# Sums of squares by ScalarE's accumulator, and a new order of steps, in a gated-memory and routed feed-forward kernel

## The reference

```python
ctx = causal_ema(x, tau_ctx)
wg = sigmoid(concat(x, ctx) @ Wg.T + bg);  gated = x * wg
h1 = gelu(x @ Wn1.T + bn1);  mod = 0.5 + sigmoid(h1 @ Wn2.T + bn2)
traces = causal_ema(gated * mod[..., d], tau_raws[d])   # for each of 128 d
temporal = sum_d traces[d] * softmax(blend)[d]
gate = sigmoid(temporal @ Wtemp.T + btemp)
soma = gelu(x @ Wsoma.T + bsoma)
out = (soma * gate) @ Wout.T
y = (out - out.mean(-1)) / sqrt(out.var(-1) + 1e-5) * gamma + beta
scores = y @ w_router;  top_idx = top 16 of 32 tokens of each sequence
update = sigmoid(top_scores) * (gelu(y[top_idx] @ W1 + b1) @ W2 + b2)
result = x + y.at[top_idx].add(update)
```

## Time and profile before

| | |
|---|---|
| time, median of 3 runs | 190.28 us (189.97 to 190.45) |
| the profiled execution's own time | 190.07 us |
| its span in the profile | 188.0 us |
| TensorE busy, weight loads | 179.4 us (95%), 139.8 us |
| VectorE busy | 142.5 us (76%) |
| GpSimd busy | 132.3 us (70%) |
| ScalarE busy | 94.7 us (50%) |
| DMA | 5.62 MB |
| mean granted TensorE clock | 0.997 |

### The profile page before, as it was taken

The page is one execution under the profiler, slowest core; times in us unless marked ns, Lnnn a source line. Parts: engine busy times, 40 slices in busy tenths (PEclk is TensorE's granted clock), DMA queues, the critical chain, the costliest instruction groups (busy, mean ns, idle before and its releaser), DMA issues.

```text
span 188.0 us, 3687 instructions
## 1 busy us (share of the span) xinstructions
PE 179.4 (95%) x1256; PEld 139.8 (74%) x1256; DVE 142.5 (76%) x247; ACT 94.7 (50%) x172; POOL 132.3 (70%) x142
## 2 busy tenths in 40 slices
PE   6999999999999999999999999999998999997991
PEld 6777485687758677877786889767865997895981
DVE  1687978967977559988888766999799865967632
ACT  3156763645652543363623477394683916637230
POOL 7307126596887999998799889977899478809700
PEclk9999999999999999999999999999999999999998
DMA  4795000000000000000000000000100000303032
GB/s 125 186 250 145 0 2 0 5 0 0 5 0 0 0 0 3 0 0 3 2 0 3 0 0 0 3 2 0 50 11 0 2 3 0 112 3 112 0 108 59
DMA packets 12785, 5.62 MB, mean 30 GB/s; under 512 B 2880, under 2 KB 12640, under 8 KB 12768
## 3 DMA queue, kind: packets, MB, share of 16 engines
q1 hardware_dynamic: 11616, 5.20, 10.2%
q10 hardware_dynamic: 1152, 0.20, 0.6%
HBM read 3.30 MB, written 2.10 MB: 29 GB/s over the span
## 4 chain that ended last, share of the span: by engine, by line
PE 88%; DVE 4%; POOL 3%; issue 2%; ACT 0%; DVEq 0%; POOLq 0%
PE ring L996 28%; PE ring L1063 8%; PE ring L953 4%; PE ring L926 4%; PE ring L969 4%; PE ring L932 4%; PE ring L980 4%; PE ring L1023 4%; PE ring L954 4%; PE ring L1011 3%; PE ring L1003 3%; PE ring L878 2%; PE ring L1047 2%; PE ring L960 2%; PE ring L986 2%
## 5 line engine op out<-in xcount | busy, mean ns | idle before, releaser
L434 POOL TENSOR_TENSOR ctx_acc<-ctx_acc,prod 128x384 f32<-128x384 f32 (+20 forms) x75 | 81.5, 1100 | 26.1 <-DVE prod L772 21.0
L772 DVE TENSOR_TENSOR prod<-ring,gm 128x384 f32<-128x384 f32 (+20 forms) x75 | 41.7, 579 | 12.4 <-PE ring L996 9.1
L996 PE MATMUL ring<-mod_hi,decayed_lo 128*128 128x512 f32 (+12 forms) x104 | 34.6, 370 | 0.0
L996 PE MATMUL ring<-mod_lo,decayed_hi 128*128 128x512 f32 (+12 forms) x104 | 30.0, 326 | 0.0
L996 PE MATMUL ring<-mod_hi,decayed_hi 128*128 128x512 f32 (+12 forms) x104 | 30.0, 326 | 0.0
L996 PEld LDWEIGHTS ring<-mod_hi,decayed_lo 128*128 128x128 f32 x104 | 18.6, 189 | 8.8 <-issue 7.2
L996 PEld LDWEIGHTS ring<-mod_lo,decayed_hi 128*128 128x128 f32 x104 | 19.3, 189 | 1.6 <-issue 0.7
L996 PEld LDWEIGHTS ring<-mod_hi,decayed_hi 128*128 128x128 f32 x104 | 19.2, 189 | 0.9
L759 DVE TENSOR_TENSOR state<-ring,blend_w 128x1024 f32<-128x1024 f32 x16 | 18.8, 1217 | 0.5 <-PE ring L969 0.4
L1063 PEld LDWEIGHTS ring<-w_sb,gm 128*128 128x128 f32 x128 | 14.8, 192 | 1.2 <-issue 1.2
L1063 PE MATMUL ring<-w_sb,gm 128*128 128x128 f32 x128 | 15.2, 276 | 0.1
(11 more groups left out here) (162 smaller groups left out, 375.0 us busy)
## 6 DMA issues: line engine op xcount, KB each, us to landing
x_nat<-in_x_dram SPq DMA_DIRECT2D x3, 512.0 KB, 5.2
out_dram<-x_nat SPq DMA_DIRECT2D x3, 512.0 KB, 3.2
x_nat<-in_x_dram SPq DMA_DIRECT2D x2, 256.0 KB, 4.8
w_sb<-in_L_ffn_W_dram SPq DMA_DIRECT2D x2, 256.0 KB, 4.7
out_dram<-x_nat SPq DMA_DIRECT2D x2, 256.0 KB, 2.3
down<-in_cond_dram SPq DMA_DIRECT2D x2, 64.0 KB, 3.1
prod<-in_L_cond_Wg_dram ACTq DMA_DIRECT2D x1, 128.0 KB, 2.9
prod<-in_L_cond_Wsoma_dram ACTq DMA_DIRECT2D x1, 64.0 KB, 2.9
```

Of the source, the lines that this page charges most:

```text
L434: nc.gpsimd.tensor_tensor(dst, dst, packed(prod[:, n % NP, 0:width(r)], r, k), ALU.add).then_inc(acc_done, 1)
L772: nc.vector.tensor_tensor(dst, packed(slot(step), r, k), lagged(gated(r), r, k), ALU.mult).then_inc(read(step), 1)
L996: last = nc.tensor.matmul(to[:, c], w[:, k, :], src[:, c], start=(i == 0), stop=(i == len(parts) - 1))
```

## The change

Two things change. First, `out` on ScalarE squares each of its four tiles by an instruction of its own, which also sums the squares along the row into `small` (`accum_out`). The step `stats` on VectorE is gone (its names stay in the table and do nothing), and so is its wait; the sums are done when ScalarE is. Second, `ORDER` is replaced by another order of the same steps.

```diff
                 elif kind == "out":
-                    at = nth(step)
-                    if at > 1:
-                        last = [s for s in STEPS if s[0] == "stats"][at - 2]
-                        act.wait_ge(stats_done, nth(last))
-                    nc.scalar.activation(squares[:, :, :].rearrange("p (h n) e -> p h n e", h=2),
-                                         slot(step).rearrange("p (h n) -> p h n", h=2)[:, :, 0:2 * OW].rearrange(
-                                             "p h (n w) -> p h n w", w=OW)[:, :, :, 0:E], ACT.Square,
-                                         scale=E ** -0.5).then_inc(read(step), 1)
+
+                    if nth(step) > 1:
+                        act.wait_ge(stats_done, QT * (nth(step) - 1))
+                    if r >= 2:
+                        act.wait_ge(rstd_done, r - 1)
+                    for n in range(QT):
+                        at = n // 2 * BANK + n % 2 * OW
+                        nc.scalar.activation(squares[:, n, :], slot(step)[:, at:at + E], ACT.Square, scale=E ** -0.5,
+                                             accum_out=small[:, r % 2, 5, k * QT + n:k * QT + n + 1]).then_inc(stats_done, 1)
...
-                elif kind == "stats":
-
-                    dve.wait_ge(read(("out", r, k)), reads_after(("out", r, k)) - 1)
-                    if r >= 2:
-                        dve.wait_ge(norm_done, BEFORE[r - 1] * QT)
-                    nc.vector.tensor_reduce(small[:, r % 2, 5, k * QT:(k + 1) * QT], squares[:, :, :], AX_X,
-                                            ALU.add).then_inc(stats_done, 1)
...
 ORDER = """
-decay:0 turn_a:0 xt:0 context:0 turn_b:0 powers:0 h1:0 wg:0 soft:0 xt:1 gated:0 context:1 turn_c:0 table:0.0
+decay:0 turn_a:0 xt:0 context:0 plus_beta:0 turn_b:0 h1:0 powers:0 wg:0 soft:0 gated:0 xt:1 context:2
...
-up:3.0 score:4 up:3.1 bc:4 normed:4 turn_pick:3 tie:4 pick:4 residual:3 down:3 gather:4 scatter:3 up:4.0
+score:4 normed:4 turn_pick:3 bc:4 tie:4 pick:4 plus_beta:3 residual:3 down:3 plus_beta:4 gather:4 scatter:3
```

More of the change, by code:

```diff
@@ L78 @@
-turn_pick:2 pick:3 sum:4 gate:4 soma_gate:4 residual:2 down:2 gather:3 out:4.0 stats:4.0 var:4 scatter:2
-up:3.0 score:4 up:3.1 bc:4 normed:4 turn_pick:3 tie:4 pick:4 residual:3 down:3 gather:4 scatter:3 up:4.0
-up:4.1 residual:4 turn_pick:4 down:4 scatter:4
+decay:0 turn_a:0 xt:0 context:0 plus_beta:0 turn_b:0 h1:0 powers:0 wg:0 soft:0 gated:0 xt:1 context:2
+turn_c:0 context:1 h1:1 table:0.0 mod:0 split:0 context:4 low:0 xt:2 rw:0 turn_f:0 table:0.1 mod:1 table:0.2
+table:0.3 split:1 early:0 unit:0.0 wg:1 context:3 gated:1 unit:0.3 xt:3 h1:2 low:1 unit:0.8 nat:0.0 early:1
@@ new lines @@
+turn_d:0 unit:0.11 unit:0.12 unit:1.0 unit:0.13 unit:1.12 unit:1.7 unit:1.9 mod:2 plus_beta:1 unit:0.1
+unit:1.6 state:0.0 xt:4 wg:2 gated:2 turn_e:0 unit:0.4 unit:1.4 unit:0.10 unit:0.9 unit:1.13 wg:3 gated:3
+unit:0.6 nat:1.0 h1:4 h1:3 carry:0.0 unit:0.14 unit:0.5 unit:0.15 nat:1.1 back:0.0 unit:1.10 mod:3 unit:0.2
+unit:0.7 split:2 early:2 sum:0 unit:1.5 state:1.0 unit:1.1 soma:0 gate:0 low:2 unit:1.3 soma_gate:0
+carry:1.0 unit:1.8 unit:2.0 nat:2.0 unit:2.15 unit:1.15 unit:1.11 unit:1.14 unit:1.2 unit:2.3 state:2.0
@@ new lines @@
+unit:2.1 split:3 low:3 soma:1 out:0.0 unit:2.8 state:1.1 wg:4 back:1.0 stats:0.0 var:0 carry:2.0 mod:4
+gated:4 score:0 unit:2.11 unit:2.13 unit:2.12 bc:0 carry:1.1 normed:0 tie:0 pick:0 unit:2.6 unit:2.5
+back:2.0 unit:2.14 unit:3.0 nat:2.1 unit:3.1 back:1.1 unit:2.4 early:3 state:2.1 soma:2 sum:1 unit:3.4
+unit:2.10 turn_pick:0 unit:3.14 gather:0 nat:3.1 unit:3.7 nat:3.0 unit:3.12 ffn_w:0 state:3.0 residual:0
+gate:1 soma_gate:1 plus_beta:2 carry:2.1 unit:2.9 unit:2.2 unit:2.7 split:4 up:0.0 low:4 back:2.1 sum:2
@@ new lines @@
+out:1.0 unit:3.2 up:0.1 unit:4.0 unit:4.7 out:1.1 state:3.1 gate:2 unit:4.1 soma_gate:2 early:4 stats:1.0
+stats:1.1 unit:4.9 carry:3.0 unit:3.5 nat:4.0 unit:3.13 out:2.0 state:4.0 var:1 score:1 normed:1 unit:4.15
+down:0 unit:3.15 unit:3.9 unit:3.3 unit:3.6 out:2.1 bc:1 tie:1 soma:4 unit:3.8 carry:3.1 stats:2.0 stats:2.1
+pick:1 var:2 unit:4.13 back:3.0 carry:4.0 gather:1 score:2 soma:3 unit:4.8 back:3.1 unit:3.11 back:4.0
+unit:3.10 unit:4.10 normed:2 sum:3 scatter:0 unit:4.4 unit:4.6 bc:2 up:1.0 turn_pick:1 tie:2 pick:2 gate:3
@@ L81 @@
+residual:1 unit:4.2 unit:4.5 up:1.1 soma_gate:3 gather:2 out:3.0 out:3.1 stats:3.0 unit:4.3 unit:4.12
+stats:3.1 var:3 score:3 up:2.0 normed:3 unit:4.14 down:1 unit:4.11 up:2.1 bc:3 sum:4 scatter:1 turn_pick:2
+tie:3 pick:3 gate:4 soma_gate:4 residual:2 down:2 gather:3 out:4.0 stats:4.0 scatter:2 up:3.0 up:3.1 var:4
+score:4 normed:4 turn_pick:3 bc:4 tie:4 pick:4 plus_beta:3 residual:3 down:3 plus_beta:4 gather:4 scatter:3
+up:4.0 residual:4 up:4.1 turn_pick:4 down:4 scatter:4
 """
```

5 lines of the change are left out of this document (2 added, 3 removed).

## The result

The changed kernel took 194.0 us (median of four executions: 192.73, 192.75, 195.24, 197.64), the kernel before 190.13 beside it. The change is slower, by 1.4 to 2.2%, as forecast. The profiled execution is one of the two of 192.7: span 190.8 us against 188.0.

The account below looks back on a forecast made before the run. TensorE, busy for 95% of the span, was taken to bound the kernel. Start +2.5, middle -0.8 and -0.6, end +2.2 gave +3.3 us, so 193.6 us against the median of 190.28; 8-in-10 range 190.7 to 196.3.

Parts of the forecast that it names:

- The start: `plus_beta:0` waits for `gamma_r` and delays the tables; TensorE waits 2.9 us before its first unit, net +2.5 us.
- +0.5 us before `var:4`: Squares of `out:4` on the path: four ScalarE pairs of 0.46 us, 1.85 us instead of 1.32.
- 4 x 0.27 if the reads overlap: Lower bound for the squares of `out:4`: 1.1 us, so -0.2 us before `var:4`.
- hidden as said: ScalarE's longer squares, 10 us over eight `out` steps, costed at nothing where units on TensorE cover them.
- The middle: The wait before `bc:2` goes, -0.8 us; fewer narrow steps, -0.6 us; new waits costed at nothing.
- -0.6 us: TensorE crosses between step shapes 55 times instead of 61, at 0.11 us each.
- The end: Before `bc:4`: score and spread both held by GpSimd, squares later, `turn_pick:3` filling 0.4 us; +2.2 us.
- two ways in which I let the spread go: Spread of `score:4`: held by gapless GpSimd instructions, tail +2.2 us; or mostly slipping through, +0.1 us.
- Only the start stalls: Rival: the spread of `score:4` gets through between two GpSimd instructions; 191.5 us, chance 0.15.
- new waits in the middle: Rival: `gate:2` or `gate:3` waits for its sum, or ScalarE is late for `down`; 195 to 196.5 us, chance 0.13.
- no difference: Rival: start stall of half the size, net +1.3, spread through, middle as forecast; 190.3 us, chance 0.08.
- Faster: Rival: TensorE's three old waits go and no new one comes; 187.1 us, or some 188; chance 0.11.

Follow-up runs that it names:

- beta0_later: The changed kernel with only `plus_beta:0` moved, from the start to behind the first add (`unit:0.3`): 191.61 us, 1.0056 times the kernel before.
- beta_only_wait: Changed kernel, `plus_beta:3` and `plus_beta:4` moved behind `residual:2`, `gamma_r` given its own semaphore so `plus_beta:0` doesn't wait for it: 188.43 us, 0.9906 times the kernel before.
- acc_only: The kernel before with only the squares summed by ScalarE's accumulator, in the old order: 190.14 us, 0.9997 times the kernel before.
- both_moved: The changed kernel with `plus_beta:0` moved behind `unit:0.3`, and `plus_beta:3` and `plus_beta:4` behind `residual:2`: 188.09 us, 0.9902 times the kernel before.
- residual3_late: `both_moved` with `residual:3` on GpSimd also waiting for the spread of `score:4`: 187.33 us, 0.9847 times the kernel before.
- unit0_behind_wg1: `residual3_late` with `unit:0.0` behind `wg:1` in the table instead of ahead of it: 187.09 us, 0.9846 times the kernel before.
- order_dve_sums: The order of `both_moved` with the old code's sums on VectorE, three `stats` steps set ahead of `out` steps: 188.19 us, 0.9896 times the kernel before.
- both_beta4_late: `both_moved` with `plus_beta:4` alone set behind `var:4` again: 189.34 us, 0.9958 times the kernel before.
- after_again: The changed kernel run once more with nothing edited: 196.74 us, 1.0263 times the kernel before.

## Why the prediction was right, point by point

- **The start.** Right in each step and in its size: line 422 at 16.09 (16.0 forecast), tables at 17.31 (17.3), first unit at 22.55 (22.5), wait 2.37. It was forecast at 2.9; TensorE came 0.5 us later than in the profile of before, and the wait took that up. Against the other kernel that makes +2.5, as forecast. `beta0_later` and `beta_only_wait` show the cause from two sides.
- **The first part.** The term "+0.5 us before `var:4`" was mis-sized. I took 0.46 us for a square and its read from the one such pair in the trace, which had no second one behind it. In a row they come every 0.25 us, the read lying beside the next square: -0.17 measured, in the profile of the change and in `acc_only`. The bound "4 x 0.27 if the reads overlap" was the right one. ScalarE's total rose by 4 us, not 10, and was hidden as said.
- **The middle.** The wait before `bc:2` is gone (-0.79). No new wait came between 30 and 165 us: TensorE is busy for 134.98 of these 135 us. The "-0.6 us" for fewer narrow steps is not shown, though the sum came out as if it were there: what is left of the span's difference after the waits and the start of `xt:0` is -0.42 here, and -0.31, -0.66 and -0.43 in `both_moved`, `residual3_late` and `unit0_behind_wg1`, but -0.02 in `order_dve_sums`, which has the same TensorE order and as few narrow steps. Its price per step was misread too: of the 0.11 us that the earlier trace rows show behind a narrow step, 0.08 stand behind a full-size step as well. What the some -0.4 us are is open, and that they came near the forecast's -0.6 is in part luck.
- **The end.** Right in mechanism: score 2.34 and spread 2.22 us, both held, `turn_pick:3` ahead of `bc:4`. TensorE's wait grew by 1.51 and not 2.2 us, and the difference is the squares' 0.67. Of the two ways in which I let the spread go, the gap decides, as `both_beta4_late` and `residual3_late` show. The Trainium skill has the rule that a VectorE instruction with two SBUF inputs contends with a GpSimd one that reads SBUF ("SBUF — State Buffer", section "Who interferes with whom"), and the traces agree, with 0.16 us for a score alone and 2.34 beside line 422.
- **The sum.** +2.8 on the span, +2.6 on the time in undisturbed clock (192.7), where I had +3.3: the squares -0.67, and the rest within 0.2 of the forecast.
- **What the forecast lacked.** It named the waits' length as their only price. The median of 194.0 lies nearer to my 193.6 than 192.7 does, but that is luck, for a reason that I didn't have: with the waits TensorE ran at 1.2 GHz for some microseconds in most executions. In `after_again` that took the median to 196.7, above my range. The mean clock accounts for what the ten executions of the two runs differ in, to 1.6 us, as said above. The Trainium skill describes that a wait can put TensorE back to half its clock ("TensorE: Matmul & The Clock Gate", section "HAM oscillation — how this bites in real kernels"). The stretches above agree with it, though in `after_again` the first work behind the wait (0.48 us at 22.86, beside 0.47 in the profile of the changed kernel) was not yet slower, and it should have stood among my rivals.
- **The rivals.** "Only the start stalls", "new waits in the middle" and "no difference" didn't occur. "Faster" did once the two conditions that it named were met (a start wait under 1 us, a spread that slips through): 188.1 in `both_moved`, and it had said 187.1 to 188.
